# A fourth row buffer in the expert stage, and the first mixture's later row sends placed over half a stage

## The chip, the core and the metric

The kernel runs on one core of a Trainium2 chip. The metric is the device time of one execution in microseconds (us), from start to end of the program. Beside it stand a profile and a trace of one execution; its span runs from the first to the last instruction. The engines are TensorE (PE; its weight loads are PEld), VectorE (DVE), ScalarE (ACT), GpSimd (POOL) and SyncE (SP), which issues most DMAs.

## The reference

x has 8 batches of 512 tokens of 128 features (4096 tokens). Two layers run one after the other, each as x = x + s(xn) * silu(g(xn)) with xn the layer-normed x.

- Layer 0: s is an attention with 16 heads of 8 features, a residual, a layer norm and a projection. g is a mixture of 64 experts of hidden size 64, of which each token takes 8 with sigmoid weights, plus a shared expert.
- Layer 1: s is a gated recurrence over the sequence (gates f, i, o, z; c = f*c + i*z; h = o * tanh(layernorm(c))). g is a mixture of 8 experts of hidden size 512, of which each token takes 2, with a capacity of 1281 places per expert:

```
flat_e = k_idx.reshape(-1)
onehot = one_hot(flat_e, E)
rank = take_along_axis(cumsum(onehot, axis=0) - 1, flat_e[:, None], axis=1)[:, 0]
keep = rank < capacity
buf = zeros((E, capacity, H)).at[flat_e, slot].add(dispatched)
h = silu(einsum('ech,ehf->ecf', buf, w1)); out_buf = einsum('ecf,efh->ech', h, w2)
```

So the first mixture's output decides the router of the second, and every token's normed row must be sent to a place in the table of its two experts before an expert can run.

## The kernel before, in words

Three phases follow each other.

1. `attention_phase` (to about 500 us of the span): layer 0's attention, the next phase's weights and gates.
2. `mixture_phase` (500 to 949 us): the first mixture, called the first mixture in the title. It works in eight stages of 512 tokens (stage 0 to 7). A stage has 33 units (q = 0 to 32): 32 pairs of experts and the shared expert. For a unit, PE forms the hidden layer with three fp16 matmuls (lines 1758 to 1760), ACT applies silu (line 1652), DVE multiplies by the gates (line 1855), ACT writes the high fp16 part (`m_hidh`, line 1646), POOL writes the low part (`m_hidl`, line 1583) and, four units after the first three, PE adds the unit to the output with three matmuls (lines 1738 to 1740). The low part of some units is made by DVE in place of POOL (line 1872): those are q = 4, 10, 16, 22, 28 in stages 1, 3 and 5, and q = 2, 6, 9, 13, 16, 20, 24, 28, 31 in the even ones (a similar list in stage 7). PE's product with a unit waits for its low part.

   Beside the units of stage s runs the end of stage s - 1's tokens, by tables of places q (`PE_AT`, `ACT_AT`, `DVE_AT`, `POOL_AT`): output, layer norm (POOL's `inverse_std`, lines 1602 and 1604, at q = 6), router, ranks, and the places of the rows (`slots` at q = 24). In stages 1, 3 and 5 a part of the recurrence of layer 1 runs too. The rows themselves go out by eight indirect DMAs per 512 tokens, issued by POOL (`send`, line 1593): three at q = 27, 29, 31 of the stage after theirs (`SENT_AT`) and five in the next stage at the places q of `SENT_LATER`, through `further`. POOL's order is fixed: at each q first the unit's low part, then `follow` (sends of `SENT_AT`, `inverse_std`), then the recurrence, then `further`. After stage 7 come a tail of router and recurrence work (903 to 949 us) and the last thirteen sends. A row buffer is not written again before its sends have landed (semaphore `sent`), which is asked in `norm` at q = 10 and in `slots` at q = 24, a full stage after the last of the later sends.
3. `expert_phase` (949 us to the end): layer 1's mixture. Each of the 8 experts has 1287 places, loaded as one block of rows (117 partitions of 11 rows of 144 numbers, 724 KB) into one of `XBUFS` = 3 buffers, and worked through in three blocks (4, 4 and 3 tiles of 117 rows), each with four groups of 3 + 3 matmuls. `rows_turned` transposes a block's rows one block ahead (line 2212) and waits for the load; `result_rows` on DVE weighs the results (line 2285), and POOL sends them to their tokens with one indirect DMA per tile (line 2150), eleven for an expert. SP issues the loads (`load_places`, lines 168 and 172): those of experts 0 to 2 at the end of the mixture phase, then in the expert phase first the two big loads for the final sum (`kept_rows`, line 177), and then expert e's when the results of expert e - 3 have been made and have landed. The last part sums what came back and writes the output.

`done` are four output buffers of the last part; `yT` are two buffers that hold a block's result before it is transposed.

Of the kernel before, what the change touches and what calls it, by code (L numbers as in the profile page):

```python
# [13 lines left out]
ALU = mybir.AluOpType  # L14
ACT = mybir.ActivationFunctionType
AX = mybir.AxisListType
F32 = mybir.dt.float32
# [4 lines left out]
P = 128  # L22
D = 128
# [3 lines left out]
TILES = TOK // P  # L27
# [6 lines left out]
LN_EPS = 1e-5  # L34
# [4 lines left out]
CT = 11  # L39
CR = -(-CAPACITY // CT)  # L40
PLACES = CT * CR
REC = D + 2 * E1
NOWHERE = 1 << 20
XBUFS = 3
WS = 64.0

QS = 16.0
# [78 lines left out]
class Ahead:  # L126
# [27 lines left out]
            w.append(ctx.enter_context(nc.sbuf_tensor(f"p_{n}1", [P, NQ[1], P], F16)))  # L154

    def place_buffers(self, nc, ctx):
        self.rows_in = [ctx.enter_context(nc.sbuf_tensor(f"p_rows{k}", [CR, CT, REC], F32)) for k in range(XBUFS)]
        self.x_in = [ctx.enter_context(nc.semaphore(f"p_x_in{k}")) for k in range(XBUFS)]
        self.first_in = ctx.enter_context(nc.semaphore("p_first_in"))


def load_places(sp, scratch, pre, e):
# [12 lines left out]
def kept_rows(sp, scratch, kept, kept_in):  # L175
    for n in ("x1", "s1"):
        sp.dma_start(kept[n][:], scratch[n].rearrange("(n p t) d -> p n (t d)", p=P, t=TILES)).then_inc(kept_in, 16)
# [56 lines left out]
def attention_phase(nc, io, scratch, ident, consts_ready, pre):  # L234
    with ExitStack() as ctx:
# [3 lines left out]
        def sem(name):  # L239
            return ctx.enter_context(nc.semaphore(name))  # L240
# [13 lines left out]
        meanvar = sb("a_meanvar", [P, TILES, 2])  # L254
        rstd = sb("a_rstd", [P, TILES, 1])
        vareps = sb("a_vareps", [P, TILES, 1])
        cvareps = sb("a_cvareps", [P, 1])
# [26 lines left out]
        cmv = sb("a_cmv", [P, 2])  # L284
# [21 lines left out]

        w_in = sem("a_w_in")
        x_in = [sem(f"a_x_in{p}") for p in range(2)]
        ln_eps, c_eps = sem("a_ln_eps"), sem("a_c_eps")
        ln_stats, ln_aggr, ln_rstd = sem("a_ln_stats"), sem("a_ln_aggr"), sem("a_ln_rstd")  # L310
        xn_ready = sem("a_xn_ready")
        misc_full, misc_free = sem("a_misc_full"), sem("a_misc_free")
# [18 lines left out]
        c_stats, c_aggr, c_rstd, cn_done = (sem(f"a_c_{n}") for n in ("stats", "aggr", "rstd", "norm"))  # L331
# [256 lines left out]
        def _(pool):  # L588
            def inverse_std(n):
                pool.wait_ge(ln_aggr, n.at(TILES, TILES))  # L590
                apart(pool)
                pool.tensor_scalar(vareps[:], meanvar[:, :, 1:2], LN_EPS, None, ALU.add).then_inc(ln_eps, 1)
                pool.wait_ge(ln_eps, n.at(1, 1))
                pool.tensor_tensor(rstd[:], vareps[:], neghalf[:, 0:TILES].unsqueeze(2), ALU.pow
                                   ).then_inc(ln_rstd, 1)

            def normalise(n):
                pool.wait_ge(ln_rstd, n.at(1, 1))
                apart(pool)
                for t in range(TILES):  # L600
                    pool.tensor_scalar(xn[n.p][:, t, :], xin[n.p][:, t, :], meanvar[:, t, 0:1], rstd[:, t, :],
                                       ALU.subtract, ALU.mult).then_inc(xn_ready, 1)
# [70 lines left out]
            def context_norm(s, tau):  # L673
                pool.wait_ge(c_aggr, s.at(TILES, tau + 1))
                apart(pool)
                pool.tensor_scalar(cvareps[:], cmv[:, 1:2], LN_EPS, None, ALU.add).then_inc(c_eps, 1)
                pool.wait_ge(c_eps, s.at(TILES, tau + 1))
                pool.tensor_tensor(crstd[:], cvareps[:], neghalf[:, 0:1], ALU.pow).then_inc(c_rstd, 1)
                if not (s.first() and tau == 0):

                    pool.wait_ge(misc_full, misc_use(s, f"cn{tau - 1}" if tau else "cn3p") + 1)
                pool.wait_ge(c_rstd, s.at(TILES, tau + 1))
                apart(pool)
                pool.tensor_scalar(cn[:], res[:], cmv[:, 0:1], crstd[:], ALU.subtract, ALU.mult
                                   ).then_inc(cn_done, 1)
# [264 lines left out]
        def _(dve):  # L950
# [9 lines left out]
                    dve.bn_aggr(meanvar[:, t, :], stats[:, t, :]).then_inc(ln_aggr, 1)  # L960

            def normalise(n):
                dve.wait_ge(ln_rstd, n.at(1, 1))
                for t in range(TILES):
                    dve.tensor_scalar(xn[n.p][:, t, :], xin[n.p][:, t, :], meanvar[:, t, 0:1], rstd[:, t, :],
                                      ALU.subtract, ALU.mult).then_inc(xn_ready, 1)
# [263 lines left out]

SENT_AT = (27, 29, 31)
SENT_AT_LAST = (25, 26, 28)
SENT_LATER = (1, 3, 5, 7, 9)
SENDS = len(SENT_AT) + len(SENT_LATER)

PER = {"unit": NQ, "gate": (2 * 16 * GROUPS // SLOTS, 0), "once": (1, 0), "prep": (1, 0),
# [115 lines left out]
def mixture_phase(nc, io, scratch, ident, pre):  # L1352
    with ExitStack() as ctx:
# [136 lines left out]
        @block.sync  # L1490
        def _(sp):
            def load(s):
                sp.dma_start(xh[s.p][:], scratch["xh0"][:, s.tokens()]).then_inc(st_in[s.p], 16)
                sp.dma_start(xl[s.p][:], scratch["xl0"][:, s.tokens()]).then_inc(st_in[s.p], 16)

            def load_ep(s):
                sp.dma_start(sT[s.p][:], scratch["s0"][:, s.tokens()]).then_inc(ep_in[s.p], 16)
                x_t = io["x"].rearrange("(n p) d -> p n d", p=P)
                sp.dma_start(xres[s.p][:], x_t[:, s.tiles(), :]).then_inc(ep_in[s.p], 16)

            sp.wait_ge(wsplit, 2 * JOBS)
            for k in range(RAWS):
                load_chunk(sp, io, pre, JOBS + 1 + k)
            load(Turn(0, 0, 1))
            sp.wait_ge(pre.s_out, 16 * BATCH)
            load_ep(Turn(0, 0, 0))
            load_ep(Turn(0, 0, 1))

            def unit(s, q):
                if q < UNITS and q % GROUP == GROUP - 1:  # L1510

                    g = q // GROUP + SLOTS
                    to = s if g < GROUPS else s.following()
                    if to:
                        sp.wait_ge(mul_done, s.n("unit", q + 1))
                        apart(sp)
                        load_gate_pair(sp, scratch, pre, to, g % GROUPS)
                k = job_at(s, q)
                if k is not None and k + RAWS < JOBS:
                    sp.wait_ge(wsplit, 2 * (JOBS + 1 + k) + 4)  # L1520
                    load_chunk(sp, io, pre, JOBS + 1 + k + RAWS)

            def follow(b, q):

                nxt = b.after_next()
                if q == 0 and nxt:
                    sp.wait_ge(up_done, b.n("unit", NQ[b.layer]))
                    apart(sp)
                    load(nxt)
                if q == 9:  # L1530
                    sp.wait_ge(x_kept, b.n("once", 1))
                    out_t = scratch["x1"].rearrange("(n p) d -> p n d", p=P)
                    sp.dma_start(out_t[:, b.tiles(), :], xnew[:]).then_inc(x_out, 16)
                    if nxt:
                        load_ep(nxt)
                if q == 12:
                    sp.wait_ge(xn_ready, b.n("tiles", TILES))
                    apart(sp)
                    out_t = scratch["last"].rearrange("(n p) d -> p n d", p=P)
                    sp.dma_start(out_t[:, b.tiles(), :], rec[b.p][:, :, 0:D]).then_inc(xn_out, 16)  # L1540
            def store_s(b):
                sp.wait_ge(sR_rel, b.n("once", 1))
                apart(sp)
                out_t = scratch["s1"].rearrange("(n p) d -> p n d", p=P)
                sp.dma_start(out_t[:, b.tiles(), :], srow[b.p][:]).then_inc(s_out[b.p], 16)

            def recur(b, q):
                if q == STORE_AT:
                    store_s(b)

            run_stages(sp, unit, follow, recur)
            for q in range(NQ[0]):
                follow(LAST, q)
            store_s(stage_of(PUT_OFF[0]))
            for p in range(2):
                sp.wait_ge(sent[p], 16 * SENDS * PASSES)
            for e in range(XBUFS):
                load_places(sp, scratch, pre, e)
            for late in PUT_OFF[1:]:
                store_s(stage_of(late))  # L1560
            sp.wait_ge(x_out, 16 * BATCH)
            sp.wait_ge(xn_out, 16 * BATCH)
# [500 lines left out]
OUTS = 4  # L2063


def expert_phase(nc, io, scratch, ident, pre):
    with ExitStack() as ctx:
        def sb(name, shape, dt=F32):
            return ctx.enter_context(nc.sbuf_tensor("e_" + name, shape, dt))
# [5 lines left out]
            return ctx.enter_context(nc.psum_tensor("e_" + name, shape, F32))  # L2075

        wuh, wul, wdh, wdl = pre.wuh[1], pre.wul[1], pre.wdh[1], pre.wdl[1]
        rows_in, x_in = pre.rows_in, pre.x_in
        xh, xl = ([sb(f"{n}{k}", [P, 512], F16) for k in range(2)] for n in ("xh", "xl"))
        hidh, hidl = sb("hidh", [P, XRING, 512], F16), sb("hidl", [P, XRING, 512], F16)  # L2080
# [3 lines left out]
        held = [t.rearrange("p (k b x) -> p k b x", k=K1, x=TILES * D) for t in (  # L2084
            pre.gates[:].rearrange("p s t -> p (s t)"), pre.raw[:].rearrange("p a n x -> p (a n x)"))]
        pick = [held[n // 4][:, :, n % 4, :] for n in range(PIECES)]
        done = [sb(f"done{j}", [P, TILES * D]) for j in range(OUTS)]

        hps, yps = ps("h", [P, XBANKS, 512]), ps("y", [P, 2, 512])
        xps, ops = ps("x", [P, 512]), ps("o", [P, 512])  # L2090
# [26 lines left out]
        def _(sp):  # L2117
            for p in range(2):
                sp.wait_ge(pre.s1_out[p], 16 * PASSES)
            kept_rows(sp, scratch, kept, kept_in)  # L2120
            for e in range(XBUFS, E1):
                sp.wait_ge(row_done, NB * (e - XBUFS + 1))
# [272 lines left out]
```

## Time and profile before

| | us |
|---|---|
| median of 3 runs | 1145.13 |
| lowest, highest | 1142.84, 1145.99 |
| the profiled execution's own time | 1142.7 |
| its span, first to last instruction | 1141.0 |

| engine | busy us | share of the span |
|---|---|---|
| PE | 995.5 | 87% |
| DVE | 846.0 | 74% |
| ACT | 769.5 | 67% |
| POOL | 643.6 | 56% |

The time of a run is a little longer than the span of its instructions. Busy shares are averages over three phases with different limits; what an edit is worth is read from the stretch that it touches. In the lists of instructions below, a row gives start, duration, engine, line, operation, output <- inputs, shapes, and in brackets how long the engine stood idle before it and what ended that.

### The profile page before, as it was taken

How to read it: one execution, taken by the hardware profiler on the slowest of the kernel's cores; microseconds unless marked ns; L12 is line 12 of the kernel's file. 1: busy time of each engine (PE TensorE's matmuls, PEld its weight loads, DVE VectorE, ACT ScalarE, POOL GpSimd, SP SyncE). 2: the span in 40 equal slices, each digit the busy share in tenths (PEclk: the TensorE clock that was granted, in tenths of full speed). 3: DMA queues.
4: the chain of work that ended last, by engine and by line, in shares of the span. 5: the costliest groups of instructions: out<-in, count | busy, mean ns of one | idle time of the engine just before them, and what ended most of it. 6: DMA issues, size and time to landing. Idle time of an engine off the chain costs nothing. (4 is left out here: it accounts for less than half of the span.)

```text
span 1141.0 us, 18343 instructions
## 1 busy us (share of the span) xinstructions
PE 995.5 (87%) x5032; PEld 421.4 (37%) x5032; DVE 846.0 (74%) x1678; ACT 769.5 (67%) x1460; POOL 643.6 (56%) x781
## 2 busy tenths in 40 slices
PE   4699999998999999869999999999999977878860
PEld 3133333332333322123444444444444334545430
DVE  4598888897989898748776777777677785565555
ACT  1077777776777777657777877787887646666651
POOL 6444536353545423346668778786977640655555
PEclk9999999999999999879999999999999987999985
DMA  2553935132322311669868777776776325112126
GB/s 59 94 97 97 202 87 115 44 57 52 47 61 37 70 20 46 180 186 254 225 178 234 203 200 193 227 215 179 219 210 198 91 105 192 54 51 84 55 96 238
DMA packets 102379, 149.78 MB, mean 131 GB/s; under 512 B 18216, under 2 KB 72088, under 8 KB 101838
## 3 DMA queue, kind: packets, MB, share of 16 engines
q1 hardware_dynamic: 95470, 139.65, 46.0%
q0 software_dynamic: 6272, 8.94, 2.6%
q8 instruction: 37, 0.61, 0.2%
q10 hardware_dynamic: 544, 0.13, 0.2%
q14 instruction: 56, 0.46, 0.1%
HBM read 109.44 MB, written 40.04 MB: 131 GB/s over the span
## 5 line engine op out<-in xcount | busy, mean ns | idle before, releaser
L809 ACT ACTIVATE a_probs<-a_score 128x512 f32<-128x512 f32 x512 | 291.9, 598 | 118.9 <-PE a_score L890 111.8
L985 DVE TENSOR_REDUCE a_mx<-a_mxps 128x2 f32<-128x1024 f32 x256 | 306.5, 1211 | 51.1 <-PE a_mxps L881 46.4
L1583 POOL TENSOR_TENSOR m_hidl<-m_hid,m_hidh 128x512 f16<-128x512 f32 x203 | 234.2, 1169 | 84.7 <-ACT m_hidh L1646 78.0
L1652 ACT ACTIVATE m_h<-m_h 128x512 f32<-128x512 f32 (+1 forms) x264 | 153.4, 581 | 60.3 <-PE m_h L1760 54.2
L1855 DVE TENSOR_TENSOR m_hid<-m_h,p_gates 128x512 f32<-128x512 f32 x196 | 134.0, 688 | 68.1 <-ACT m_h L1652 63.2
L902 PE MATMUL a_ops<-a_probs,a_vst 128*32 128x512 f32 x1024 | 138.4, 613 | 0.5 <-ACT a_probs L809 0.5
L1646 ACT ACTIVATE m_hidh<-m_hid 128x512 f16<-128x512 f32 x203 | 126.1, 621 | 13.2 <-DVE m_hid L1855 12.9
L2150 POOL DMA_INDIRECT t_picked<-e_yrow,p_rows x77 | 76.7, 996 | 84.4 <-DVE e_yrow L2285 59.7
L1738 PE MATMUL m_y<-m_hidh,p_wdh 128*128 128x512 f16 (+1 forms) x264 | 100.4, 380 | 21.3 <-POOL m_hidl L1583 19.7
L890 PE MATMUL a_score<-a_qstack,a_kstack 128*128 128x512 f16 x256 | 98.1, 389 | 6.4 <-ACT a_probs L809 3.3
L2298 DVE SCALAR_TENSOR_TENSOR e_hidl<-e_h,e_hidh 128x468 f16<-128x468 f32 (+1 forms) x96 | 57.4, 603 | 62.2 <-ACT e_hidh L2166 51.4
L890 PE MATMUL a_score<-p_gates,p_raw 128*128 128x512 f16 x256 | 98.5, 385 | 3.2 <-DMA p_gates<-a_mT 0.9
L1740 PE MATMUL m_y<-m_hidl,p_wdh 128*128 128x512 f16 (+1 forms) x264 | 100.0, 379 | 0.0
L1739 PE MATMUL m_y<-m_hidh,p_wdl 128*128 128x512 f16 (+1 forms) x264 | 100.0, 379 | 0.0
L881 PE MATMUL a_mxps<-p_raw,p_gates 126*128 126x512 f16 x256 | 83.2, 409 | 14.8 <-DVE a_mx L985 7.1
L2185 ACT ACTIVATE e_h<-e_h 128x468 f32<-128x468 f32 (+1 forms) x96 | 51.1, 532 | 45.7 <-PE e_h L2236 38.0
L609 POOL TENSOR_SCALAR a_mscaled<-a_mx 128x16 f32<-128x16 f32 x32 | 8.9, 277 | 127.4 <-DVE a_mx L985 127.3
L881 PE MATMUL a_mxps<-a_kstack,a_qstack 126*128 126x512 f16 x256 | 76.4, 379 | 0.0
L1593 POOL DMA_INDIRECT t_slots<-m_rec,m_slot x64 | 64.3, 1005 | 20.5 <-issue 11.8
L1855 DVE TENSOR_TENSOR m_h<-m_h,p_gates 128x512 f32<-128x512 f32 x60 | 41.9, 698 | 28.5 <-ACT m_h L1652 26.8
L890 PEld LDWEIGHTS a_score<-a_qstack,a_kstack 128*128 128x128 f16 x256 | 24.2, 97 | 104.2 <-ACT a_probs L809 89.8
L890 PEld LDWEIGHTS a_score<-p_gates,p_raw 128*128 128x128 f16 x256 | 24.8, 97 | 99.5 <-ACT a_probs L809 84.7
(293 smaller groups left out, 1915.6 us busy)
## 6 DMA issues: line engine op xcount, KB each, us to landing
p_gates<-t_cw SPq DMA_DIRECT2D x256, 256.0 KB
t_slots<-p_blank SPq DMA_DIRECT2D x8, 723.9 KB
p_rows<-t_slots SPq DMA_DIRECT2D x7, 723.9 KB
t_qparts<-a_qparts SPq DMA_DIRECT2D x32, 128.0 KB
t_picked<-p_blank SPq DMA_DIRECT2D x8, 512.0 KB
p_raw<-up SPq DMA_DIRECT2D x8, 512.0 KB, 5.5
p_raw<-down SPq DMA_DIRECT2D x8, 512.0 KB, 5.5
a_xin<-x SPq DMA_DIRECT2D x8, 256.0 KB, 5.0
```

What stands on the lines that cost most here:

```text
L809: act.activation(probs[:, kt % 2, g, :], score[:, g % 2, :], ACT.Exp, scale=SCALE / (QS * QS)).then_inc(exp_done, 1)
L881: op = pe.matmul(mxps[:, j % 2, k, :], stack[0][where.p][0:ZROWS, qt, g, at, :], stack[1][where.p][0:ZROWS, :, g, at, :], start=True, stop ...
L890: pe.matmul(score[:, g % 2, :], stack[1][s.p][:, kt, g, tau, :], stack[0][s.p][:, :, g, tau, :], start=True, stop=True).then_inc(score_ful ...
L902: op = pe.matmul(ops[GT * g:GT * g + GT, :], vst[half][:, tau * NG + g, kt, :], probs[:, kt % 2, g, :], start=(kt == 0), stop=(kt == KT - ...
L985: dve.tensor_reduce(mx[ahead % 2][:, j // 2, g:g + 2], mxps[:, j % 2, :, :], AX.X, ALU.max).then_inc(mx_done, 1)
L1583: pool.tensor_tensor(hidl[0:r0, k % r, :], hid[0:r0, k % r, :], hidh[0:r0, k % r, :], ALU.subtract).then_inc(lo_done[0], 1)
L1646: act.activation(hidh[0:r0, k % r, :], gated, ACT.Copy).then_inc(hi_done, 1)
L1652: act.activation(h, h, ACT.Silu, scale=1.0 / WS).then_inc(silu_done, 1)
L1738: pe.matmul(yps[:], wdh[n][0:r0, q, :], hidh[0:r0, r, :], start=(q == 0), stop=False)
L1739: pe.matmul(yps[:], wdl[n][0:r0, q, :], hidh[0:r0, r, :], start=False, stop=False)
L1740: pe.matmul(yps[:], wdh[n][0:r0, q, :], hidl[0:r0, r, :], start=False, stop=(q == NQ[n] - 1)).then_inc(dn_done, 1)
L1855: dve.tensor_tensor(gated, h, gates[:, q % (SLOTS * GROUP), :], ALU.mult).then_inc(mul_done, 1)
```

## The change

There are four edits.

- In the first mixture the later five of the eight sends of a stage's rows are issued at q = 1, 4, 10, 13, 16 and no longer at q = 1, 3, 5, 7, 9.
- The expert stage has four row buffers and no longer three. The fourth is placed in the expert phase's own memory. Experts 0 to 2 are loaded at the same point as before; expert 3's rows are loaded as the expert stage begins, ahead of the two big loads; expert e's (e from 4) when expert e - 4 is done.
- To make room, two of the four output buffers of the last part share the memory of `yT`, which is free by then.
- In the attention and its layer norm two semaphores are merged into their neighbours; the instructions and the waits stay the same in number and order.

```
-XBUFS = 3
+XEARLY, XBUFS = 3, 4
...
-        self.rows_in = [... f"p_rows{k}" ... for k in range(XBUFS)]
+        self.rows_in = [... f"p_rows{k}" ... for k in range(XEARLY)]
+
+    def more_places(self, nc, ctx):
+        self.rows_in += [... f"e_rows{k}" ... for k in range(XEARLY, XBUFS)]
...
-                pool.tensor_scalar(vareps[:], meanvar[:, :, 1:2], LN_EPS, None, ALU.add).then_inc(ln_eps, 1)
-                pool.wait_ge(ln_eps, n.at(1, 1))
+                pool.tensor_scalar(vareps[:], meanvar[:, :, 1:2], LN_EPS, None, ALU.add).then_inc(ln_rstd, 1)
+                pool.wait_ge(ln_rstd, n.at(2, 1))
...
-SENT_LATER = (1, 3, 5, 7, 9)
+SENT_LATER = (1, 4, 10, 13, 16)
...
-            for e in range(XBUFS):
+            for e in range(XEARLY):
                 load_places(sp, scratch, pre, e)
...
+        pre.more_places(nc, ctx)
...
-        done = [sb(f"done{j}", [P, TILES * D]) for j in range(OUTS)]
+        done = yT + [sb(f"done{j}", [P, TILES * D]) for j in range(len(yT), OUTS)]
...
             for p in range(2):
                 sp.wait_ge(pre.s1_out[p], 16 * PASSES)
+            for e in range(XEARLY, XBUFS):
+                load_places(sp, scratch, pre, e)
             kept_rows(sp, scratch, kept, kept_in)
```

## Rows read from the trace of the kernel before

**Rows 1.** The page: busy time, share and instructions of each engine.
```profile
PE 995.5 (87%) x5032; PEld 421.4 (37%) x5032; DVE 846.0 (74%) x1678; ACT 769.5 (67%) x1460; POOL 643.6 (56%) x781
```
**Rows 2.** Busy time by stretch, stages 2 and 3: stretch, its length, busy us, PEclk, DMA, GB/s.
```profile
600.70:648.50 47.80, 45.93 (x224) 21.25 (x223) 34.81 (x84) 38.67 (x73) 38.26 (x36) 1.00 0.79 220
648.50:702.30 53.80, 50.13 (x237) 23.19 (x236) 38.99 (x98) 41.35 (x77) 41.48 (x40) 1.00 0.70 194
```
**Rows 3.** Waits in stages 2 to 7: us in total, times, longest us.
```profile
PE m_y L1738 <- POOL m_hidl L1583: 14.7, 17, 1.8
```
**Rows 4.** Instructions in order, PE: units 7 and 8 of stage 2, then of stage 3.
```profile
617.95 0.39 PE L1738 MATMUL m_y<-m_hidh,p_wdh 128*128 128x512 f16 x1 [0.68 <-POOL m_hidl L1583]
...
620.40 0.39 PE L1738 MATMUL m_y<-m_hidh,p_wdh 128*128 128x512 f16 x1 [0.99 <-POOL m_hidl L1583]
...
665.25 0.39 PE L1738 MATMUL m_y<-m_hidh,p_wdh 128*128 128x512 f16 x1 [0.56 <-POOL m_hidl L1583]
...
667.71 0.39 PE L1738 MATMUL m_y<-m_hidh,p_wdh 128*128 128x512 f16 x1 [0.99 <-POOL m_hidl L1583]
```
**Rows 5.** Instructions in order, POOL, stage 2.
```profile
611.70 2.29 POOL L1583 TENSOR_TENSOR m_hidl<-m_hid,m_hidh 128x512 f16<-128x512 f32 x2
614.16 0.99 POOL L1593 DMA_INDIRECT t_slots<-m_rec,m_slot  x1 [0.17 <-issue]
615.40 0.22 POOL L1602 TENSOR_SCALAR m_vareps<-m_mv 128x4 f32<-128x4 f32 x1 [0.25 <-issue]
...
616.74 1.15 POOL L1583 TENSOR_TENSOR m_hidl<-m_hid,m_hidh 128x512 f16<-128x512 f32 x1
618.06 1.09 POOL L1593 DMA_INDIRECT t_slots<-m_rec,m_slot  x1 [0.17 <-issue]
619.17 1.17 POOL L1583 TENSOR_TENSOR m_hidl<-m_hid,m_hidh 128x512 f16<-128x512 f32 x1
```
**Rows 6.** Instructions in order, DVE: the last step before POOL's inverse_std, stages 2, 3.
```profile
614.92 0.38 DVE L1900 BATCH_NORM_AGGREGATE m_mv<-m_stats 128x2 f32<-128x6 f32 x4
...
661.75 0.38 DVE L1900 BATCH_NORM_AGGREGATE m_mv<-m_stats 128x2 f32<-128x6 f32 x4
```
**Rows 7.** Instructions in order, POOL: before unit 7 of stage 3, then of stage 7.
```profile
661.56 1.18 POOL L1583 TENSOR_TENSOR m_hidl<-m_hid,m_hidh 128x512 f16<-128x512 f32 x1
662.69 0.24 POOL L1602 TENSOR_SCALAR m_vareps<-m_mv 128x4 f32<-128x4 f32 x1
...
865.88 0.22 POOL L1602 TENSOR_SCALAR m_vareps<-m_mv 128x4 f32<-128x4 f32 x1 [1.05 <-DVE m_mv L1900]
```
**Rows 8.** Instructions in order, PE: its first product with unit 11, stage 2.
```profile
624.73 0.38 PE L1738 MATMUL m_y<-m_hidh,p_wdh 128*128 128x512 f16 x1
```
**Rows 9.** Instructions that touch the table of rows: duration ns min/median/max, first and last start.
```profile
L1593 POOL DMA_INDIRECT t_slots<-m_rec,m_slot x64: 966/991/1230, 597.7 to 931.5; - x64
```
**Rows 10.** Busy time by stretch, experts 0, 1, 6 and 7.
```profile
953.00:967.50 14.50, 14.23 (x77) 7.89 (x75) 9.62 (x16) 12.13 (x28) 0.00 (x0) 0.91 0.77 281
967.50:987.70 20.20, 17.24 (x97) 10.41 (x95) 12.12 (x21) 13.53 (x32) 11.16 (x11) 0.92 0.09 23
...
1065.00:1082.10 17.10, 15.58 (x96) 9.39 (x95) 9.75 (x17) 11.95 (x27) 10.91 (x12) 1.00 0.25 74
1082.10:1101.80 19.70, 15.63 (x83) 8.73 (x82) 9.25 (x17) 13.05 (x30) 9.95 (x11) 0.91 0.10 28
```
**Rows 11.** Instructions in order: SP's loads of experts 3 to 7; PE's transposes for expert 3.
```profile
988.51 79.00 SPq L172 DMA_DIRECT2D p_rows<-t_slots  x5
...
998.59 0.57 PE L2212 MATMUL e_x<-ident,p_rows 117*128 117x117 f32 x4
```
**Rows 12.** Waits in the expert stage up to 1104 us.
```profile
ACT e_h L2185 <- PE e_h L2236: 38.0, 32, 3.5
```
**Rows 13.** Instructions that touch one of the two big loads' buffers (columns as in rows 9).
```profile
L2314 DVE TENSOR_TENSOR e_h<-e_h,e_s x8: 689/690/700, 1125.5 to 1135.1; 128x512 f32<-128x512 f32 x8
```
**Rows 14.** Busy time by stretch: the first 6 us of the expert stage.
```profile
949.70:955.70 6.00, 4.53 (x16) 2.54 (x17) 0.89 (x2) 1.70 (x4) 0.00 (x0) 0.50 0.65 200
```

More of the change, by code:

```diff
@@ L156, in place_buffers @@
     def place_buffers(self, nc, ctx):
-        self.rows_in = [ctx.enter_context(nc.sbuf_tensor(f"p_rows{k}", [CR, CT, REC], F32)) for k in range(XBUFS)]
+        self.rows_in = [ctx.enter_context(nc.sbuf_tensor(f"p_rows{k}", [CR, CT, REC], F32)) for k in range(XEARLY)]
         self.x_in = [ctx.enter_context(nc.semaphore(f"p_x_in{k}")) for k in range(XBUFS)]
         self.first_in = ctx.enter_context(nc.semaphore("p_first_in"))
+    def more_places(self, nc, ctx):
+        self.rows_in += [ctx.enter_context(nc.sbuf_tensor(f"e_rows{k}", [CR, CT, REC], F32)) for k in range(XEARLY, XBUFS)]
 def load_places(sp, scratch, pre, e):
@@ L308, in attention_phase @@
         x_in = [sem(f"a_x_in{p}") for p in range(2)]
-        ln_eps, c_eps = sem("a_ln_eps"), sem("a_c_eps")
         ln_stats, ln_aggr, ln_rstd = sem("a_ln_stats"), sem("a_ln_aggr"), sem("a_ln_rstd")
@@ L597, in normalise @@
             def normalise(n):
-                pool.wait_ge(ln_rstd, n.at(1, 1))
+                pool.wait_ge(ln_rstd, n.at(2, 2))
                 apart(pool)
@@ L675, in context_norm @@
                 apart(pool)
-                pool.tensor_scalar(cvareps[:], cmv[:, 1:2], LN_EPS, None, ALU.add).then_inc(c_eps, 1)
-                pool.wait_ge(c_eps, s.at(TILES, tau + 1))
+                pool.tensor_scalar(cvareps[:], cmv[:, 1:2], LN_EPS, None, ALU.add).then_inc(c_rstd, 1)
+                pool.wait_ge(c_rstd, s.at(2 * TILES, 2 * tau + 1))
                 pool.tensor_tensor(crstd[:], cvareps[:], neghalf[:, 0:1], ALU.pow).then_inc(c_rstd, 1)
@@ L681, in context_norm @@
                     pool.wait_ge(misc_full, misc_use(s, f"cn{tau - 1}" if tau else "cn3p") + 1)
-                pool.wait_ge(c_rstd, s.at(TILES, tau + 1))
+                pool.wait_ge(c_rstd, s.at(2 * TILES, 2 * tau + 2))
                 apart(pool)
@@ L962, in normalise @@
             def normalise(n):
-                dve.wait_ge(ln_rstd, n.at(1, 1))
+                dve.wait_ge(ln_rstd, n.at(2, 2))
                 for t in range(TILES):
```

## The prediction

> **What bounds the kernel now.** I read the page first: PE is busy for 87% of the span, the next engine for 74% [rows 1]. A share over three phases decides nothing, so the second view is busy time by stretch, for the stages of the first mixture. Stage 2 lasts 47.80 us, of which PE is busy 45.93; stage 3 lasts 53.80 with 50.13 [rows 2]. PE is the bound there, and the most an edit of another engine can give is PE's idle time: 1.87 us in an even stage and 3.67 in an odd one. The third view, the waits over stages 2 to 7, says who owns it: PE's first matmul of a unit's second half (line 1738) stood idle for 14.7 us, 17 times, for POOL's low parts [rows 3]. The fourth view, PE in order of time, says where: at unit 7 and at unit 8 of a stage. In stage 2 the gaps are 0.68 and 0.99 us, in stage 3 0.56 and 0.99 [rows 4]. The other four stages repeat this (even stages and stage 7 like stage 2, stage 5 like stage 3). That is 4 x 1.67 + 2 x 1.55 = 9.8 of the 14.7 us; the rest are gaps elsewhere, one of 1.8 us near q = 24 of each odd stage (the recurrence) and a few beside the sends at the end of stage 7, which no edit moves.
>
> Why units 7 and 8: POOL chained, one low part starts 1.12 us after the other (2.29 for two, each of 1.15 to 1.17), and a send costs 0.99 us and some 0.3 around it [rows 5]. PE takes about 1.3 us for a unit (44 us for 33). A send on top of a low part makes 2.4, and old places at every second q leave POOL no room to catch up before inverse_std at q = 6.
>
> **The first mixture, step by step.** In each of the stages 2 to 7 four of the five later sends move.
>
> Stage 2 as the pattern of the four stages with the even list. The send at q = 5 (614.16) goes, but inverse_std does not move with it: it starts at 615.40, and the last aggregate that it needs ends at 614.92 + 0.38 = 615.30 [rows 5, 6]. In stage 7, where POOL is ahead, it waits 1.05 us for the same [rows 7]. So low part 7 still starts at 616.74, and PE's 0.68 us at unit 7 stays. Then the send at q = 7 (618.06) is gone: low part 8 starts about 617.86 and ends about 619.03. PE, without its gap, wants it at 620.40 - 0.99 = 619.41 [rows 4, 5]. The gap of 0.99 goes whole, with 0.3 us to spare. Gain: 0.99 in each of four stages, 3.96.
>
> Stage 3 as the pattern of the two others. There unit 6 belongs to POOL, and inverse_std starts at 662.69, right after it, while the aggregate ended at 661.75 + 0.38 = 662.13 [rows 6, 7]. Without the send at q = 5 low part 6 is done sooner and inverse_std starts about 662.23: 0.46 earlier. The gap at unit 7 falls from 0.56 to about 0.1, that at unit 8 goes: 0.45 + 0.99 = 1.44. Bounds: 0.99 if the low part of unit 6 has no earlier input, 1.55 if both gaps go. Twice 1.44 is 2.88.
>
> What the sends cost at their new places. q = 4 follows unit 3 or 4, in POOL's order where the send of q = 3 was. At q = 10, 13 and 16 the lag is gone. In the odd stages 10 and 16, in the even ones 13 and 16 are units whose low part DVE makes, so POOL has a free slot of 1.3 us for a send of 1.3. The one at q = 10 of an even stage comes on top of low part 10: that part starts about 619.0, the send about 620.3, low part 11 about 621.3 and ends 622.5. PE took that unit at 624.73 [rows 8] and, without the gap of 0.99, wants it at 623.74. Margin 1.2 us, cost nothing. At q = 13 of an odd stage PE itself is slowed by recurrence work. Lower bound of the gain if a gap of that kind opened once a stage: its length could be what a gap is now, 0.99, which would undo the even stages. I take 0, since the margin is above it.
>
> Nothing is lost in buffers: the norm and the places that rewrite a row buffer come a stage after the last send. The three sends at q = 27 to 31 and the thirteen after stage 7 keep their places. The sum is 3.96 + 2.88 = 6.8 us, with 3.9 and 9.8 as bounds (odd stages giving nothing; every gap of rows 4 gone).
>
> *A rule weighed.* All 64 sends took between 0.966 and 1.230 us, at places with every mix of DVE work beside them [rows 9]. The Trainium skill, SBUF — State Buffer, section "SBUF: two separate sides", says that a POOL-issued DMA can be starved while DVE holds a port that the two share; its example goes from some 0.62 us to 3.1 us. It speaks against moving sends to q = 10 to 16, beside DVE's norm and router. By the page 2.5 us more on a send would eat the margin and the gain; by the rows a send can grow by 0.24 us, which the margins hold, and no send here shows the long case.
>
> **The expert stage.** A buffer more helps if PE waits for rows. It does not: the loads of experts 3 to 7 are issued at 988.51 to 1067.2, and PE first takes expert 3's rows at 998.59 with no idle time noted [rows 11], ten microseconds after the issue. The others repeat it. The change moves these issues one expert earlier: that of expert 3 to about 951 less the shift, the others to the old places of their predecessors; the place at 1067 falls empty. Do the loads slow what runs beside them? Expert 0 ran in 14.5 us under 281 GB/s. Expert 1, with no load of rows beside it, took 20.20 us, expert 7, also without, 19.70, and expert 6, with one, 17.10 [rows 10]. The long experts come from something else: ACT waits 38.0 us for the first matmuls' results [rows 12]. So cost and gain are 0. Bounds: expert 6 losing its load becomes like 1 or 7 (+3.1), or the others gain what the load share costs at most, as far as 18.3 to 20.2 of the middle experts spread (-2).
>
> Queue order on SP: the new load stands ahead of the two big ones, 0.7 MB before 4, about 3 us at 281 GB/s. They are first needed at 1125.5 [rows 13], 160 us later. The shared output buffers are written only after all experts are through; the merged semaphores move no instruction. Both 0.
>
> **The sum.** The profiled execution took 1142.7 (span 1141.0 and 1.7 around it) and would take 1135.9. It lies 2.4 below the median of 1145.13, so for the median: 1145.1 - 6.8 = 1138.3 us.
>
> **Rivals.**
> - *The freed time is taken back within the stage* (the layer norm, at q = 10, and the recurrence near 24 set the pace): only some 2.5 us remain, 1142.6. For it: unit 7 is already such a case, and q = 24 has a gap of 1.8. Against: those chains hang on PE's own products and shift with it.
> - *The experts without a load beside them are slower* (1 and 7 against 6): 3.1 back, 1141.4.
> - *The load does cost something in the experts*: 2 to 3 us more, 1135.7.
> - *The sends grow by 0.24 at the new places*, once on the path per stage: 6 x 0.24 = 1.4, 1139.7. The rule above would be its extreme.
> - *Slower.* PE enters the expert stage with a granted clock of 0.50, its lower level of 1.2 GHz, and keeps it for 6 us; then 2.4 GHz comes [rows 14]. If with the moved start and the longer traffic the lower level lasted through expert 0, its 14.5 us at 0.91 would be 14.5 x 0.91 / 0.50 = 26.4, 11.9 more: 1150.2. It decides from 10.2 us of loss on, that is if six sevenths of the expert run so. Against: nothing PE does in the 15 us before changes.
> - *The change not doing what it says*: sends at 10 to 16 could be issued late in a bunch; POOL's fixed order excludes it.
>
> **How the numbers follow.** Forecast 0.52, freed time taken back 0.14, slower experts 0.12, load cost 0.11, slower 0.07, longer sends 0.04. A measurement of this kernel tells 0.3%, 3.4 us, from no change. Faster: forecast, load cost, longer sends and a bit of the slower experts, 0.69. Same: the case taken back and most of the slower experts, 0.23. Slower: 0.08. The range runs from the load case with the upper bound of the first mixture, 1133.5, to the case taken back, 1143.5.
>
> **What would show it.** Stages 2, 4, 6 and 7 shorter by 1.0 us and stages 3 and 5 by 1.4; PE with a gap of about 0.7 at unit 7 of the even stages and none at unit 8; inverse_std still right behind the aggregate; in the experts five issues of loads with the last near 1041, and expert lengths still of 17 to 20 us. Wrong it would be if unit 7's gap went too, if a gap opened at units 11 to 17, or if an expert's length followed its load.

## The result and the profile after

| | us |
|---|---|
| before, median of 5 (lowest, highest) | 1145.13 (1142.84, 1147.12) |
| changed, median of 5 (lowest, highest) | 1136.5 (1135.14, 1137.29) |
| changed over before | 0.9926, 95% interval [0.9908, 0.9944] |
| changed, the profiled execution: time, span | 1136.95, 1134.4 |
| before, the profiled execution: time, span | 1142.7, 1141.0 |

The change takes 8.6 us off the median, where 6.8 were forecast; 1136.5 lies in the stated range of 1133.5 to 1143.5. The interval of the ratio is 6.4 to 10.5 us.

The changed kernel's lines lie a little further down: 1738 is 1740 there, 1583 is 1585, 1593 is 1595, and in the expert phase about 5 are added. The first view is busy time by stretch of the changed kernel, for stages 2 and 3, to be held against [rows 2].

```profile
600.60:647.31 46.71, 45.81 (x224) 21.34 (x223) 34.80 (x84) 38.62 (x73) 38.33 (x36) 1.00 0.82 225
647.31:699.38 52.07, 49.87 (x236) 23.24 (x235) 38.89 (x98) 41.28 (x77) 41.39 (x40) 1.00 0.71 200
```

Stage 2 is 46.71 us long, where the start of one stage to the start of the next was 47.85; stage 3 is 52.07 where it was 53.71. Every engine is busy for the same time as before, within 0.3 us; what went is idle time of PE. Measured from the first matmul of one stage to that of the next, and for the tail to the first transpose of the expert stage:

| stage | 0 | 1 | 2 | 3 | 4 | 5 | 6 | 7 | tail to the experts |
|---|---|---|---|---|---|---|---|---|---|
| before | 48.10 | 52.07 | 47.85 | 53.71 | 47.83 | 53.69 | 47.84 | 51.91 | 46.2 |
| changed | 48.67 | 52.27 | 46.71 | 52.07 | 46.68 | 52.07 | 46.68 | 50.75 | 45.8 |

Stages 2 to 7 give 1.14, 1.64, 1.15, 1.62, 1.16 and 1.16, together 7.9 us. Next, PE in order, units 7 and 8 of stage 2 and then of stage 3, against [rows 4].

```profile
617.90 0.39 PE L1740 MATMUL m_y<-m_hidh,p_wdh 128*128 128x512 f16 x1 [0.69 <-POOL m_hidl L1585]
619.21 0.38 PE L1740 MATMUL m_y<-m_hidh,p_wdh 128*128 128x512 f16 x1
...
663.57 0.39 PE L1740 MATMUL m_y<-m_hidh,p_wdh 128*128 128x512 f16 x1
664.88 0.38 PE L1740 MATMUL m_y<-m_hidh,p_wdh 128*128 128x512 f16 x1
```

The gap at unit 7 of the even stage has stayed (0.69, it was 0.68), the one at unit 8 is gone in both stages (no bracket), and unit 7 of stage 3 has no noted gap (it was 0.56). A little is left there all the same: the matmul before starts at 663.11, so this one comes 0.46 us later where two in a chain are 0.22 apart, 0.24 us late. POOL in the same stretch of stage 2 and then of stage 3, against [rows 5, 7]:

```profile
611.77 0.99 POOL L1595 DMA_INDIRECT t_slots<-m_rec,m_slot  x1 [0.17 <-issue]
612.78 1.18 POOL L1585 TENSOR_TENSOR m_hidl<-m_hid,m_hidh 128x512 f16<-128x512 f32 x1
615.35 0.23 POOL L1604 TENSOR_SCALAR m_vareps<-m_mv 128x4 f32<-128x4 f32 x1 [1.39 <-DVE m_mv L1902]
615.66 1.05 POOL L1606 TENSOR_TENSOR m_rstd<-m_vareps,m_neghalf 128x4 f32<-128x4 f32 x1
616.69 3.39 POOL L1585 TENSOR_TENSOR m_hidl<-m_hid,m_hidh 128x512 f16<-128x512 f32 x3
620.24 1.09 POOL L1595 DMA_INDIRECT t_slots<-m_rec,m_slot  x1 [0.17 <-PE m_y L1742]
621.36 2.29 POOL L1585 TENSOR_TENSOR m_hidl<-m_hid,m_hidh 128x512 f16<-128x512 f32 x2
...
661.02 0.23 POOL L1604 TENSOR_SCALAR m_vareps<-m_mv 128x4 f32<-128x4 f32 x1 [0.33 <-DVE m_mv L1902]
```

With the send of q = 5 gone, POOL stands idle for 1.39 us before inverse_std, for DVE's aggregate, and starts it at the same time as before; behind it three low parts run without a send between them. In stage 3 it now waits for the aggregate too. The sends stand one by one at their new places (q = 4 at 611.77, q = 10 at 620.24). And the waits over stages 2 to 7, against the 14.7 us of [rows 3]:

```profile
PE m_y L1740 <- POOL m_hidl L1585: 7.7, 9, 1.8
```

Next, SP's loads of rows in the expert stage, and the stage itself, experts 1, 5 and 6 (against [rows 10, 11]):

```profile
942.81 0.34 SPq L175 DMA_DIRECT2D e_rows<-t_slots  x1
...
980.10 39.70 SPq L175 DMA_DIRECT2D p_rows<-t_slots  x3
1039.02 0.30 SPq L175 DMA_DIRECT2D e_rows<-t_slots  x1
```
```profile
959.13:979.27 20.14, 17.38 (x97) 10.30 (x95) 12.11 (x21) 13.52 (x32) 11.18 (x11) 0.92 0.09 23
1038.60:1058.59 19.99, 17.39 (x97) 10.39 (x95) 10.20 (x19) 13.55 (x32) 10.86 (x11) 0.91 0.24 67
1058.59:1076.85 18.26, 15.71 (x97) 9.55 (x95) 9.77 (x19) 13.25 (x31) 9.97 (x11) 1.00 0.09 23
```

The issues have moved one expert forward. The eight experts together, first to last matmul, took 157.1 us, 3.4 more than before (153.7): expert 5 is 1.7 longer, with a granted clock of 0.91 where it was 1.00 (3.4 us at the lower level of 1.2 GHz, which the profile of before does not have in that expert), expert 6, which lost its load, 1.15 longer, expert 4 0.4. So in the two profiles 7.9 us are gained in the mixture and 3.4 given back in the experts; smaller differences in the attention, stages 0 and 1 and the last part make up the rest of the 6.6 us between the two spans. In neither profile does PE stand idle before its first transpose of any of experts 1 to 7: it never waited for rows.

### The profile page after: what moved, and what is told of

Read it like the earlier page. It is cut to its first block and busy times, and to the rows that moved or that the text cites. A ratio compares the mean times of both kernels' runs of the same rounds, so it can differ in the third digit from the quotient of the medians.

```text
span 1134.4 us, 18369 instructions
## 1 busy us (share of the span) xinstructions
PE 995.1 (88%) x5032; PEld 422.3 (37%) x5032; DVE 845.8 (75%) x1678; ACT 769.6 (68%) x1460; POOL 645.1 (57%) x781
## 5 line engine op out<-in xcount | busy, mean ns | idle before, releaser
L987 DVE TENSOR_REDUCE a_mx<-a_mxps 128x2 f32<-128x1024 f32 x256 | 306.6, 1211 | 51.3 <-PE a_mxps L883 46.4
L2155 POOL DMA_INDIRECT t_picked<-e_yrow,p_rows x66 | 65.9, 999 | 74.6 <-DVE e_yrow L2290 53.9
```

The lines of the kernel that those rows point to most:

```text
L987: dve.tensor_reduce(mx[ahead % 2][:, j // 2, g:g + 2], mxps[:, j % 2, :, :], AX.X, ALU.max).then_inc(mx_done, 1)
```

## The experiments

Four groups of runs were made. The kernel before ran in each, and its median was 1114.9, 1115.3, 1142.7 and 1115.3 us. The first two groups ran on one chip, the third (one buffer fewer; three sends in a row) and the fourth on two others. These levels differ by 28 us for the same kernel; so ratios and differences are taken within a group where that is possible, and the experts' lengths are looked at in each (the last experiment).

**The sends alone.**

```
 (kernel before)
-SENT_LATER = (1, 3, 5, 7, 9)
+SENT_LATER = (1, 4, 10, 13, 16)
```

> The kernel before with the new places of the later sends alone. Theory: the whole gain is this edit. Stages 2 to 7 get shorter as in the changed kernel (1.15 us in the even ones and in stage 7, 1.63 in stages 3 and 5, together 7.9), the expert stage keeps its three buffers and its length; the time is 7 to 9 us below the kernel before. Rival: the fourth buffer carries part of the gain; then this kernel is 2 us or more slower than the changed one.

Measured: 1106.71 us, ratio 0.9928 [0.9914, 0.9941], 8.2 us less. Stages 2 to 7 as in the changed kernel to 0.03 us (46.68, 52.07, 46.67, 52.07, 46.68, 50.74). The whole gain is this edit, as far as the medians tell (8.2 us here, 8.6 and 8.7 for the changed kernel).

**The buffer alone.**

```
 (changed kernel)
-SENT_LATER = (1, 4, 10, 13, 16)
+SENT_LATER = (1, 3, 5, 7, 9)
```

> The changed kernel with the later sends back at q = 1, 3, 5, 7, 9: the fourth buffer (and the shared output buffers and merged semaphores) alone. Theory: no difference from the kernel before beyond 1.5 us either way, stage lengths as before, PE never waiting for rows. Rival: an own gain of about 2 us, or a loss of about 3 us, since in the profile of the changed kernel the eight experts together took 157.1 us where they took 153.7; then experts 4 to 7 are longer here too.

Measured: 1115.1 us, ratio 1.0003 [0.9994, 1.0013]. Stage lengths as before, experts 1 to 6 all 15.37 us long in this kernel and in the one with the sends alone, with loads beside them or without. Busy time by stretch of this kernel, experts 1 and 6 (the second has no load beside it, and the kernel with the sends alone has one there):

```profile
968.03:983.40 15.37, 15.37 (x96) 9.64 (x95) 11.83 (x21) 13.59 (x32) 11.06 (x11) 1.00 0.11 29
1044.88:1060.26 15.38, 15.38 (x96) 9.66 (x95) 10.30 (x19) 13.60 (x32) 10.86 (x11) 1.00 0.13 34
```

PE is busy in all of it. With experts of this length the fourth buffer, the shared output buffers and the merged semaphores are worth nothing and cost nothing.

**One buffer fewer.** If three suffice, when does a buffer count?

```
-XEARLY, XBUFS = 3, 4
+XEARLY, XBUFS = 2, 2
```

> The changed kernel with two row buffers, one fewer than the kernel before. From the profiles with three: the load of expert e is issued 31.5 us after the expert before it in the same buffer begins and lands 4.3 us later, and PE needs it 4 us before its expert begins, so a buffer comes round every 39.8 us. Theory: three buffers hold 3 x 15.4 = 46.1 us of work, 6.3 more than that, so a fourth is worth nothing; two hold 30.7, 9 too few, so PE waits for rows from expert 2 on, about 9 us for every second expert, and the expert stage is 25 to 29 us longer than in the changed kernel. Rival: loads are hidden in some other way and two buffers cost under 5 us.

Measured: 1221.75 us, ratio 1.0677 [1.0638, 1.0716], against 0.9926 of the changed kernel in the first comparison, which had the same level: some 85 us, three times what I had expected. PE's waits for rows (us in total, times, longest) and one stretch (from the start of expert 2 to that of expert 3) of this kernel:

```profile
PE e_x L2217 <- DMA p_rows<-t_slots: 92.7, 6, 15.9
...
994.45:1027.95 33.50, 18.38 (x97) 11.00 (x95) 12.04 (x21) 13.72 (x32) 11.07 (x11) 0.75 0.13 38
```

PE waits for rows before each of six experts, 15.5 us each, and not for every second.

Two things were wrong in my sum. First, it took the lag from an expert's start to the next load of its buffer as fixed. But PE's order is fixed: the wait for expert e's rows stands ahead of the last block of expert e - 1, whose results free the other buffer. So the wait of one expert delays the load for the next, and each expert pays the whole shortfall, not every second one. The lag was 52 to 55 us for experts 1 to 5 here. Second, I used the numbers of short experts, and this group had long ones, with which the lag in the kernel before is 40 to 41 us for experts 1 to 4. Measured for expert 3 of this kernel: 38.5 us of lag without the wait in it, 4.5 until PE has the rows, 8.2 from there to the expert's start, together 51.3, against 36.2 us of work in the two experts before it, waits left out. That leaves 15.1 where I had 9. What is right in my sum is the sign: from issue to first use there were 10 us with three buffers [rows 11], and an expert less of work ahead turns that into a wait. The granted clock was 0.75 in the mean of that stretch, and 0.65 in the 8.2 us after a wait of 15.1; the same expert without a wait, in the kernel with the sends at q = 17 to 19 of this group, ran at 1.00. One buffer fewer costs 85 us here; one more brought nothing with short experts.

**Two of the sends alone.**

```
-SENT_LATER = (1, 4, 10, 13, 16)
+SENT_LATER = (1, 3, 5, 10, 13)
```

> The changed kernel with the later sends at q = 1, 3, 5, 10, 13: only those of q = 7 and q = 9 are moved. Theory: unit 8's gap goes everywhere, 1.15 us in each of six stages, 6.9 together; unit 7's gap of 0.56 in stages 3 and 5 comes back, so the kernel is 0.9 to 1.0 us above the changed one. Rival: the sends at q = 3 and 5 weigh as much as the one at q = 7, and half of the gain is lost, 3 us or more.

Measured: 1107.11 us, ratio 0.9931 [0.9916, 0.9945]; the changed kernel in the same group 1106.59, ratio 0.992. Stages 2, 4, 6 and 7 as in the changed kernel (46.68, 46.67, 46.67, 50.74), stages 3 and 5 at 52.56 and 52.53, 0.48 longer. PE at unit 7 of stage 3 in this kernel:

```profile
664.16 0.39 PE L1740 MATMUL m_y<-m_hidh,p_wdh 128*128 128x512 f16 x1 [0.57 <-POOL m_hidl L1585]
```

So moving the sends of q = 7 and 9 carries 6.9 us of the 7.9, and moving those of q = 3 and 5 the 1.0 of the odd stages, to the term. That the 6.9 belong to the send at q = 7 follows from POOL's order and was not run by itself: the send at q = 9 comes behind low part 8, and no gap is noted at units 9 to 22 of stages 1 to 7 in the kernel before either.

**Three sends in a row, later.**

```
-SENT_LATER = (1, 4, 10, 13, 16)
+SENT_LATER = (1, 4, 17, 18, 19)
```

> The changed kernel with the later sends at q = 1, 4, 17, 18, 19: three in a row, each on top of a low part of POOL's. Theory: PE takes a low part some 1.3 us after it is made, so one send (1.3 us) fits there and the second in a row does not: a gap opens at unit 19 of stages 2, 4, 6 and 7 (0.8 us, 0.94 with the overlap) and at unit 20 of stages 3 and 5 (0.5 us, 0.66); 5 us above the changed kernel. Rival: place does not matter once the sends are clear of inverse_std at q = 6; then the time is the changed kernel's within 1 us.

Measured: 1140.0 us, ratio 0.9971 [0.9954, 0.9988], against 0.9926 of the changed kernel in the first comparison, at the same level: about 5 us above it. Even stages 47.65, 47.62 and 47.62, stage 7 51.67 (0.93 more each), odd ones 52.36 and 52.34 (0.28 more, since the gap at unit 24 fell from 1.83 to 1.4 as the one at unit 20 opened with 0.45). By the stages it is 4.3 us. POOL in stage 2 of this kernel, then PE at unit 19:

```profile
629.23 1.16 POOL L1585 TENSOR_TENSOR m_hidl<-m_hid,m_hidh 128x512 f16<-128x512 f32 x1 [1.43 <-ACT m_hidh L1648]
630.55 1.09 POOL L1595 DMA_INDIRECT t_slots<-m_rec,m_slot  x1 [0.16 <-issue]
631.67 1.18 POOL L1585 TENSOR_TENSOR m_hidl<-m_hid,m_hidh 128x512 f16<-128x512 f32 x1
633.01 0.99 POOL L1595 DMA_INDIRECT t_slots<-m_rec,m_slot  x1 [0.17 <-issue]
634.03 1.17 POOL L1585 TENSOR_TENSOR m_hidl<-m_hid,m_hidh 128x512 f16<-128x512 f32 x1
```
```profile
635.25 0.39 PE L1740 MATMUL m_y<-m_hidh,p_wdh 128*128 128x512 f16 x1 [0.78 <-POOL m_hidl L1585]
```

The first send fits in the slack, the second uses it up, and unit 19 is late. It follows that the lag is what costs, wherever in the stage it builds up, and not the nearness to inverse_std.

**inverse_std behind the low part.** What is left at unit 7 of the even stages should be POOL's order.

```
-POOL_AT = {"rstd": 6, "crstd": 23}
+POOL_AT = {"rstd": 7, "crstd": 23}
```

> The changed kernel with POOL's inverse_std at q = 7, behind the low part of unit 7. Theory: the gap that is left at unit 7 of the even stages (0.68 us, 0.84 with the overlap that the idle time leaves out) comes from POOL waiting for DVE's aggregate ahead of that low part; with the order turned it goes in stages 2, 4, 6 and 7: 3.4 us less, and none lost, since the norm that needs the result comes at q = 10. Rival: inverse_std then ends a low part later and the norm on DVE, and with it units 9 to 11, come late: no gain or a gap of about 1 us at a later unit.

Measured: 1103.18 us, ratio 0.9892 [0.9877, 0.9907]; the sends alone in this group 1106.71 us and 0.9928. That is 3.5 us less by the medians, where 3.4 were expected, and 4.2 by the stages: even ones 45.83 (0.85 less), stages 1, 3 and 5 51.81 (0.26 less each), stage 7 49.88 (0.86 less). No gap is noted at units 7 to 11 of stages 1 to 7. The theory holds; the 0.26 of the odd stages it had left out is of the size of what was still late at their unit 7 (0.24 in stage 3). Its own stage 2:

```profile
599.94:645.76 45.82, 45.63 (x225) 21.39 (x224) 34.57 (x84) 38.37 (x72) 38.32 (x36) 1.00 0.87 230
```

**And the recurrence's inverse too.**

```
-POOL_AT = {"rstd": 6, "crstd": 23}
+POOL_AT = {"rstd": 7, "crstd": 24}
```

> The changed kernel with inverse_std at q = 7 and the recurrence's inverse (crstd) at q = 24, each behind the low part of its unit and no longer ahead of it. Theory: the 1.83 us gap at unit 24 of stages 1, 3 and 5 is POOL waiting for DVE ahead of low part 24; turned round, that part is early and unit 25 inherits some 0.7 us, so 1.1 us less in each of three stages; with the 3.5 us of inverse_std the kernel is 6.5 to 7 us below the changed one. Rival: the recurrence's norm at q = 27 on DVE is late by as much and the gap only moves on to units 27 to 29: no more than 3.5 us.

> The changed kernel with inverse_std at q = 7 and crstd at q = 24, once more. Theory: its gain is all in stages 1 to 7, whose lengths repeat to 0.1 us whatever the experts do, so the ratio is that of its first run in microseconds: 15.3 us below the kernel before, whether that stands at 1115 or at 1143. Rival: with long experts part of the gain is lost behind them, 12 us or less.

Measured: 1099.96 us, ratio 0.9858 [0.9843, 0.9872], where the changed kernel had 0.992 [0.9904, 0.9936] beside it; and 1098.07 us, ratio 0.9842 [0.981, 0.9874]. That is 15.3 and 17.2 us below the kernel before (the second interval reaches from 14.1 to 21.2); the first is 6.6 below the changed kernel beside it. It is the fastest kernel here. Odd stages fall from 52.07 to 50.52 us. PE at unit 25 of stage 3, which inherits 0.54 of the 1.83 us (0.70 with the overlap, as expected):

```profile
691.28 0.39 PE L1740 MATMUL m_y<-m_hidh,p_wdh 128*128 128x512 f16 x1 [0.54 <-POOL m_hidl L1585]
```

Both groups had short experts, so what becomes of it beside long ones was not seen.

**The changed kernel again.**

> The changed kernel itself, once more, to compare with the others on one chip. Theory: the gain in microseconds is the same on any chip, 7 to 9 us, while the level depends on how long experts 1 to 7 take (15.4 us each in the three kernels run last, 17 to 25 in the first profiles of both kernels). If the experts are again long, then the gain is less certain by the 1.7 us of a clock dip. Rival: the gain is a share of the time or tied to the long experts and differs by more than 2 us.

Measured: 1106.59 us, 8.7 below the kernel before at 1115.25, ratio 0.992 [0.9904, 0.9936]; the first comparison gave 8.6 at a level 30 us higher. The gain is the same in microseconds at both levels.

**The long experts.** In both first profiles experts 1 to 7 took 17 to 25 us, in the third group too (17 to 24 in the kernel with sends at q = 17 to 19); in the other three groups 15.4 in every kernel. Seven experts at some 4 us are the 28 us between the levels. Two kernels were to tell whether the sends of the results have a part in it. In one SP issues them as plain DMAs to a table of their own, in the other POOL does (in both the results don't reach their tokens):

```
-            pool.indirect_dma_start(plane, ..., yrow[b][:, t, :], None, ...).then_inc(put[b], 16)
+            sp.dma_start(scratch["away"][CR * k:CR * k + CR, :], yrow[b][:, t, :]).then_inc(put[b], 16)
```

> The changed kernel in which the 88 sends of results are plain DMAs issued by SP to a scratch table of their own, and no longer indirect DMAs issued by POOL: the results don't reach their tokens, the bytes are the same. Experts 1 to 7 took 18.3 to 24.8 us each in the changed kernel, expert 0 14.6. Theory A: PE's completions come late while POOL issues indirect DMAs in a chain; without them experts 1 to 7 take 14.6 to 15.5 us each and ACT's wait for the first matmuls (38 us before) falls under 8; the expert stage is some 30 us shorter. Theory B: the late completions belong to the matmuls, transposes or semaphores and not to the sends: experts 1 to 7 stay at 17 to 20 us.

> The changed kernel in which POOL sends the results of the expert stage with plain DMAs to a table of their own in place of indirect ones (the results don't reach their tokens). Theory: if experts 1 to 7 take 15.4 us here in the other kernels, they do so here too, as they did with the sends issued by SP. If they are long in the others (17 to 25 us), this kernel tells whether indirect sends from POOL are needed for it: 15.4 us here would say so, 17 or more would acquit them.

> The kernel with the expert stage's sends issued by SP as plain DMAs (results don't reach their tokens), once more. In its first run the experts took 15.4 us, but so they did in every kernel of those two groups of runs, so it told nothing of the long experts (17 to 25 us) of the first profiles. If the kernel before is near 1143 us in this group, the long experts are there: theory A (the chain of indirect sends from POOL delays the completions) then expects 14.6 to 15.5 us an expert here and a time 30 us below the changed kernel's 1136; theory B (the sends have no part in it) expects 17 to 20. If the kernel before is near 1115 us, this run again tells nothing.

Measured: 1106.98 us (ratio 0.9932 [0.9916, 0.9947]), 1103.06 and 1105.38 us (the last two single runs), each in a group whose kernels all had short experts; experts 1 to 6 took 15.37 us in all three. They show that with short experts the way of the sends costs PE nothing. Of the long ones they tell nothing, and the cause of those stays open.

## Why the prediction was right

**The even stages and stage 7.** Each sub-step came as forecast: inverse_std stayed with the aggregate (615.35, right behind 614.88 + 0.38), unit 7 kept its 0.68, unit 8 lost its 0.99. What was mis-sized is the worth of a gap: a stage lost 1.15 us and not 0.99. The rows show why. Matmuls of a unit start 0.22 us apart but are noted as 0.38 long, so the noted idle time begins only some 0.16 after PE could have started the next. Unit 7 to unit 8 took 620.40 - 617.95 = 2.45 us before and 619.21 - 617.90 = 1.31 after: 1.14. Six gaps of this kind are 1.0 us of the sum. The prediction should have taken the distance between starts. For the same reason its first statement, that PE's noted idle time (1.87 us in an even stage) is the most that an edit of another engine can give, sets the limit too low: with inverse_std behind the low part as well, stage 2 came down to 45.83, 2.02 below the 47.85 of before.

**The odd stages.** Forecast 1.44, measured 1.62 to 1.64, with the same 0.16 to 0.2 missing at unit 8. The kernel with q = 1, 3, 5, 10, 13 splits it as the prediction did: 1.15 for the send at q = 7, 0.48 for those before inverse_std (0.45 forecast). So the step's terms hold one by one.

**The new places.** They cost nothing, as forecast: no gap noted at units 9 to 22 of stages 1 to 7. The margin on which it rests, room for one send on top of one of POOL's own low parts, was tested by three in a row, and the gaps came where the same arithmetic put them (unit 19, 0.78 against 0.8; unit 20, 0.45 against 0.5).

**The rule on a starved POOL DMA** (the Trainium skill, SBUF — State Buffer, section "SBUF: two separate sides") found no case here: the sends at their new places took 0.99 to 1.09 us in the rows above.

**The expert stage.** No gain and no cost by the buffer alone: ratio 1.0003 [0.9994, 1.0013]. Both bounds that I had put beside it (3.1 us lost by expert 6 without its load, 2 gained by the others) came from comparing long experts with each other, and with short ones a load beside an expert changes 0.00 to 0.01 us. Of the 3.4 us by which the first profiles differ here, 1.7 are one more clock dip of 3.4 us at half rate; the rest is put down to the scatter of long experts. That the buffer has no part in it was shown with short experts only; in the first profiles expert 6, which lost its load, was 1.15 us longer, as the rival *slower experts* says, and in the kernel with the sends at q = 17 to 19 it took 23.8 us. No run with long experts has the buffer as its only difference, so there the rival is not excluded.

**The sum.** 6.8 forecast; 7.9 by the stages; 8.6, 8.2 and 8.7 measured in three comparisons. The 0.3 to 0.8 us between stages and medians lie inside the intervals (the narrowest is 6.6 to 9.6 us) and have no cause that was shown. Of the rivals, *the freed time is taken back* fell with the stage lengths, *slower experts* and *the load does cost* with the buffer alone (for short experts), *longer sends* with the rows, and the clock in expert 0 did not stay low (that expert took 14.56 us in both profiles). *The change not doing what it says* fell with POOL's rows.

Some of the prediction's figures do not follow from their own terms. The range is said to run between two cases, but the case taken back was priced at 1142.6 and not 1143.5, and the load case with the upper bound of the first mixture gives 1145.1 - 9.8 - 2.6 = 1132.7 and not 1133.5. The result, 1136.5, lies inside by either. The 44 us for 33 units stand in no row; units in a chain start 1.30 us apart, as assumed.

## What to carry to other kernels

- An engine's idle time as the rows note it, behind pipelined matmuls, is short by the overlap (here 0.16 us a gap). Take the distance between the starts of two like instructions, once with the gap and once without it.
- When a helper engine (here POOL at 1.12 us a unit against 1.3 of PE) is given extra work of 1.3 us, ask for its lag and not for its load: one extra piece fits the slack, the next must wait for a free slot, and a step that waits for another engine belongs behind the work that is ready. Turning that order at two places gave 6.6 us more.
- A further buffer is worth nothing while the loads land before they are needed. Once they do not, a buffer less costs more than the shortfall of one round, if the wait stands in front of the work that frees the next one: here 0 us for the fourth (short experts), 85 for the third (long ones).

## What the runs showed of the hardware

The expert stage has two lengths for the same instructions, and a whole group of runs has one or the other: 15.4 us or 17 to 25 us an expert. The three groups with short experts ran on two chips and the one with long experts on a third, so the length may belong to the chip. That is not shown: no chip ran more than two groups, and of the first comparison, also long, the chip is not on record. The row that differs is ACT's wait for the hidden layer's matmuls: 38.0 us in all before [rows 12], and in the kernel with the sends alone, with short experts,

```profile
ACT e_h L2185 <- PE e_h L2236: 16.5, 48, 3.0
```

In a long expert of the kernel before, the last matmul of a group and the ACT instruction that needs it alone stand so:

```profile
1012.01 0.36 PE L2236 MATMUL e_h<-e_xh,p_wul 128*128 128x468 f16 x1
...
1015.31 0.55 ACT L2185 ACTIVATE e_h<-e_h 128x468 f32<-128x468 f32 x1 [2.88 <-PE e_h L2236]
```

The matmul is noted as over at 1012.37 and ACT starts 2.94 us later, at a granted clock of 1.00 in that expert. It happened once or twice in each of experts 1 to 7, mostly in their second block, and not in expert 0, the only one during which no results are sent out. The sends by themselves are not enough for it: in the kernel with the sends alone, whose short experts sent their results in the same way, no ACT instruction of this line began more than 1 us after its matmul's noted end. Whether they have a part in it is not settled, since the kernels in which POOL issued no indirect ones met only short experts. The long experts cost 28 us, more than three times what the change gave.
